# The experts' second products from rounded high and low parts, their weights split once and kept in DRAM

## The reference, cut to what matters

```python
logits = jnp.einsum('bnd,esd->bnes', x, phi)            # 4 experts, 256 slots each
dispatch = softmax(logits, axis=1)
combine = softmax(logits.reshape(B, N, E * S), axis=-1).reshape(B, N, E, S)
slots = jnp.einsum('bnd,bnes->besd', x, dispatch)
h = gelu(jnp.einsum('besd,edh->besh', slots, w1) + b1)   # tanh form, hidden width 768
y = jnp.einsum('besh,ehd->besd', h, w2) + b2             # the experts' second product
out = jnp.einsum('besd,bnes->bnd', y, combine)
```

## Time and profile before

| | |
|---|---|
| median of 3 runs | 876.32 us (874.78 to 877.62) |
| the profiled execution | 876.62 us, span 874.5 us |
| TensorE busy | 812.7 us (93%) |
| its weight loads | 661.5 us (76%) |
| VectorE busy | 458.6 us (52%) |
| ScalarE busy | 469.9 us (54%) |
| GpSimd busy | 185.9 us (21%) |
| moved by DMA | 15.58 MB |

### The profile page before, as it was taken

The page is one execution under the profiler, slowest core; times in us unless marked ns, Lnnn a source line. Parts: engine busy times, 40 slices in busy tenths (PEclk is TensorE's granted clock), DMA queues, the critical chain, the costliest instruction groups (busy, mean ns, idle before and its releaser), DMA issues.

```text
span 874.5 us, 14608 instructions
## 1 busy us (share of the span) xinstructions
PE 812.7 (93%) x5240; PEld 661.5 (76%) x5240; DVE 458.6 (52%) x1009; ACT 469.9 (54%) x961; POOL 185.9 (21%) x257
## 2 busy tenths in 40 slices
PE   1989989979998989989998999999999999999998
PEld 0866766666685669878887589976989589986988
DVE  4878697687877854566663730156102730155001
ACT  4968568568767733345654643455233633455132
POOL 3150022014000022235500530035000540035000
PEclk9989999999999979999999999999999999999999
DMA  7010000001000010001101100000000000000000
GB/s 211 1 30 14 1 16 24 0 0 36 0 1 1 1 45 12 12 13 49 38 1 64 64 1 1 1 18 0 0 0 18 0 0 0 0 18 1 1 1 19
DMA packets 12854, 15.58 MB, mean 18 GB/s; under 512 B 5328, under 2 KB 10704, under 8 KB 12688
## 3 DMA queue, kind: packets, MB, share of 16 engines
q1 hardware_dynamic: 10800, 9.56, 3.5%
q0 software_dynamic: 2016, 5.51, 2.2%
HBM read 13.49 MB, written 1.57 MB: 17 GB/s over the span
## 4 chain that ended last, share of the span: by engine, by line
PE 77%; DVE 9%; ACT 7%; issue 4%; DMA 1%; SPq 1%; POOL 0%; DVEq 0%; ACTq 0%; POOLq 0%
PE ps L221 19%; PE ps L1602 14%; PE ps L1517 6%; PE ps L1246 6%; PE ps L1617 5%; PE ps L1164 4%; PE ps L1336 4%; PE ps L1144 3%; DVE area L283 2%; ACT area L1066 2%; PE ps L1152 2%; ACT area L951 2%; PE ps L1124 1%; PE ps L1542 1%; PE ps L1204 1%
## 5 line engine op out<-in xcount | busy, mean ns | idle before, releaser
L1602 PE MATMUL ps<-area 128*128 128x192 f32 x768 | 127.4, 326 | 0.0
L1602 PEld LDWEIGHTS ps<-area 128*128 128x128 f32 x768 | 124.8, 190 | 2.0 <-issue 0.5
L221 PE MATMUL ps<-xs,ws 128*128 128x512 f32 x460 | 120.7, 412 | 5.4 <-DVE xs L511 3.7
L221 PE MATMUL ps<-ws,wx 128*128 128x512 f32 x480 | 116.1, 397 | 1.3 <-DVE ws L832 1.3
L1092 ACT ACTIVATE area<-ps,bcol 128x512 f32<-128x512 f32 x96 | 65.7, 689 | 86.6 <-PE ps L221 86.6
L843 DVE TENSOR_TENSOR area<-ps,area 128x384 f32<-128x384 f32 x32 | 17.9, 558 | 177.8 <-PE ps L1602 177.8
L221 PEld LDWEIGHTS ps<-ws,wx 128*128 128x128 f32 x480 | 89.2, 188 | 22.8 <-DVE ws L832 3.0
L221 PEld LDWEIGHTS ps<-xs,ws 128*128 128x128 f32 x460 | 87.0, 195 | 25.4 <-issue 6.6
L951 ACT ACTIVATE area<-ps,nm 112x196 f32<-112x196 f32 (+1 forms) x240 | 85.8, 442 | 19.5 <-DVE nm L646 19.5
L423 POOL TENSOR_TENSOR area<-area,dstat 128x512 f32<-128x512 f32 x32 | 38.0, 1198 | 250.7 <-DVE dstat L786 250.7
L646 DVE TENSOR_REDUCE nm<-ps 112x4 f32<-112x784 f32 (+1 forms) x72 | 62.7, 874 | 28.7 <-PE ps L1144 23.7
(11 more groups left out here) (176 smaller groups left out, 1339.7 us busy)
## 6 DMA issues: line engine op xcount, KB each, us to landing
stage<-in_wall POOLq DMA_DIRECT2D x42, 128.0 KB, 2.4
area<-in_w2e SPq DMA_DIRECT2D x1, 2304.0 KB, 8.4
out<-xres SPq DMA_DIRECT2D x4, 384.0 KB, 2.6
xres<-in_x SPq DMA_DIRECT2D x1, 1152.0 KB, 6.8
area<-in_wall SPq DMA_DIRECT2D x2, 512.0 KB, 6.2
area<-in_w2a SPq DMA_DIRECT2D x1, 576.0 KB, 3.8
room<-in_rel SPq DMA_DIRECT2D x4, 128.0 KB, 5.0
xres<-in_x SPq DMA_DIRECT2D x1, 384.0 KB, 3.2
```

The source lines that it names most:

```text
L221: last = mm(out_, l, r, start=n == 0, stop=n == len(pairs) - 1)
L1602: last = mm(ps[:, 4 + b, s * D:s * D + D], hTd[:, m, b * T + s * P:b * T + s * P + P], w2x[:, e * MC + m, :], start=m == 0, stop=m == MC - 1)
```

## The change

The gelu's result and the second weights are split in a rounded high part and the rounded rest. A second product of a tile becomes, for each of six blocks, one matmul of the high part with both parts of the weights side by side (384 columns) and one of the low part with the high weights (192 columns), all in float32r. The products with the high weights land in columns 0 to 191 of a PSUM bank, the product with the low weights in 192 to 383, and VectorE adds both to the bias in two additions (`add_up`). The product of the two low parts isn't computed.

ScalarE computes the gelu twice: once rounded to SBUF (`high`), once in full into the PSUM bank that held the hidden block, from which VectorE subtracts the high part to get `low`. The bank is free for the next hidden block only then. TensorE puts the first two hidden blocks of the next expert ahead of an expert's outputs. The parts have no room in SBUF for all experts: GpSimd loads the raw weights of an expert during each of the four rounds of the causal attention, splits them and writes both parts to DRAM (`keep_parts`), and SP fetches them for each expert of each pair into one of two buffers (`fetch_w2`). The scaling of the next images is put between the experts 0 and 1, the transposes for them behind the outputs of experts 2 and 3, and ScalarE's copies into expert 3 and behind it, ahead of the exponentials. The buffers `stage` and `area` get a second name in the rounded format at the same place. The diff, cut:

```diff
+        (dd, dt_, _, ct, bc, _, b2row) = views([
             (2, 2, NE * NS), (4, 2, T), (ST * 2,), (ST, N), (N,), (NE * MC, D), (NE, D)])
         yy = area[:, 0:2 * ST * (D + 1)].rearrange("p (b s d) -> p b s d", b=2, d=D + 1)
-        hTd = area[:, 2 * ST * (D + 1):2 * ST * (D + 1) + MC * N].rearrange("p (a b) -> p a b", b=N)
+        HAT = 2 * ST * (D + 1)
+        W2AT = 4 * NE * NS + 8 * T + 2 * ST + ST * N + N
+        w2s = rounded[:, W2AT:W2AT + NE * MC * D].rearrange("p (e c) -> p e c", e=2)
+        W2C = MC * 2 * D
+        raw = area[:, 0:MC * D].rearrange("p (m d) -> p m d", d=D)
+        parts = rounded[:, MC * D:MC * D + W2C]
+        w2_kept = nc.dram_tensor("w2_kept", [P, NE, W2C], F32, kind="Internal").ap()
+
+        def high(e, m):
+
+            v_ = xs[:, m, N:2 * N] if m < 2 and e % 2 else rounded[:, HAT + m * N:HAT + m * N + N]
+            return v_.rearrange("p (b t) -> p b t", b=2)
+
+        def low(e, m):
+
+            if m < 2 and e % 2:
+                return stage_r[:] if m else xs[:, 2, N:2 * N].rearrange("p (b t) -> p b t", b=2)
+            if m < 4:
+                return ws[:, 3, m * N:m * N + N].rearrange("p (b t) -> p b t", b=2)
+            return ws[:, 2 * m - 8:2 * m - 6, NE * 2 * NS:NE * 2 * NS + T]
         slots = [ws[:, k, 0:NE * 2 * NS] for k in range(3)]
...
             sp.wait_ge(o_res, 1 + 4 * PAIRS)
-            sp.dma_start(w2x, w2e).then_inc(ld_w2, 16)
-            sp.dma_start(b2row, b2r).then_inc(ld_w2, 16)
+            sp.dma_start(b2row, b2r).then_inc(ld_b2, 16)
+
+            def fetch_w2(k):
+
+                if k >= 2:
+                    sp.wait_ge(d_y, 1 + 4 * k)
+                sp.dma_start(w2s[:, k % 2].bitcast(F32), w2_kept[:, k % NE]).then_inc((ld_w2_even, ld_w2_odd)[k % 2], 16)
+
+            sp.wait_ge(w2_out, 16 * NE)
+            for k in range(2):
+                fetch_w2(k)
             for it in range(PAIRS):
+                for k in range(NE * it + 2, min(NE * it + 6, NE * PAIRS)):
+                    fetch_w2(k)
                 sp.wait_ge(d_res, 1 + NT * (it + 1))
...
+            def fetch_raw(e):
+
+                pool.dma_start(raw, w2e[:, e * MC:e * MC + MC, :]).then_inc(ld_raw, 16)
+
+            def keep_parts(e):
+
+                pool.wait_ge(ld_raw, 16 * (e + 1))
+                if e:
+
+                    pool.wait_ge(w2_out, 16 * e)
+                hi, lo = (parts.rearrange("p (m h d) -> p m h d", m=MC, h=2)[:, :, h, :] for h in range(2))
+                nc.gpsimd.tensor_copy(hi, raw).then_inc(w2_hi, 1)
+                pool.wait_ge(w2_hi, e + 1)
+                nc.gpsimd.tensor_tensor(lo, raw, hi.bitcast(F32), ALU.subtract).then_inc(w2_lo, 1)
+                pool.wait_ge(w2_lo, e + 1)
+                pool.dma_start(w2_kept[:, e], parts.bitcast(F32)).then_inc(w2_out, 16)
+                if e + 1 < NE:
+                    fetch_raw(e + 1)
+
             for ph in range(1, 4):
                 for n in range(PAIRS):
...
+                    if ph == 2:
+                        if n == 0:
+
+                            pool.wait_ge(b_res, 1 + 2 * PAIRS)
+                            fetch_raw(0)
+                        keep_parts(n)
             dispatch_combine(PAIRS - 1)
...
+
+            def add_up(it, e, g):
+
+                n = it * 4 * NE + 4 * e + g
+                dve.wait_ge(d_y, 5 + n + 1)
+                y_ = yy[:, g // 2, 2 * e + g % 2, 0:D]
+                V.tensor_tensor(y_, ps[:, 4 + g % 2, 0:D], b2row[:, e, :], ALU.add).then_inc(d_yo, 1)
+                dve.wait_ge(d_yo, n + 1)
+                V.tensor_tensor(y_, ps[:, 4 + g % 2, D:2 * D], y_, ALU.add).then_inc(d_ye, 1)
+
...
+                front = it + (3 * PAIRS + 1), it + 1, NT
                 if nxt:
-                    front_norm(it + (3 * PAIRS + 1), it + 1, NT, [(d_st, 1 + 4 * it + 4)])
+                    front_stats(*front)
                 for e in range(NE):
-                    for b in range(2):
-
-                        dve.wait_ge(d_y, 1 + it * 2 * NE + 2 * e + b + 1)
-                        if e + b == 0:
-                            V.memset(yy[:, :, :, D:D + 1], 1.0)
-                        V.tensor_tensor(yy[:, b, 2 * e:2 * e + 2, 0:D],
-                                        ps[:, 4 + b, 0:2 * D].rearrange("p (s d) -> p s d", d=D),
-                                        b2row[:, e, :].unsqueeze(1).broadcast_to([P, 2, D]), ALU.add).then_inc(d_ye, 1)
+                    for m in range(MC):
+                        n = it * NE * MC + e * MC + m
+
+                        dve.wait_ge(d_gelu, 1 + n + 1)
+                        V.tensor_tensor(low(e, m), ps[:, (e * MC + m) % 4, :].rearrange("p (b t) -> p b t", b=2),
+                                        high(e, m).bitcast(F32), ALU.subtract).then_inc(d_hl, 1)
+                        if e and m < 4:
+                            add_up(it, e - 1, m)
+                    if e == 0:
+                        dve.wait_ge(ld_b2, 16)
+                        V.memset(yy[:, :, :, D:D + 1], 1.0)
+                    if nxt and e < 2:
+                        front_scale(*front, range(2 * e, 2 * e + 2), [(d_st, 1 + 4 * it + 4)])
+                    if e == 3:
+                        for g in range(4):
+                            add_up(it, e, g)
                     if nxt and e == 3:
                         front_split(it + (3 * PAIRS + 1), NT, (d_l, ST * it + ST))
                 for k in range(2):
...
-                    if nxt and e in (1, 2):
-                        front_turned_part(it + (3 * PAIRS + 1), 0, e - 1)
-
-                    act.wait_ge(d_y, 1 + it * 2 * NE + 2 * e)
                     for m in range(MC):
+                        if nxt and e == 3 and m == 2:
+                            front_turned_part(it + (3 * PAIRS + 1), 0, 0)
                         act.wait_ge(d_h, it * NE * MC + e * MC + m + 1)
-                        A.activation(hTd[:, m, :], ps[:, (e * MC + m) % 4, :], ACT.Gelu_apprx_tanh,
-                                     bias=bcol[:, E1B + e * MC + m:E1B + e * MC + m + 1]).then_inc(d_gelu, 1)
+
+                        if m in (0, 2):
+                            act.wait_ge(d_y, (1 if m == 0 else 5) + it * 4 * NE + 4 * e)
+                        hidden = ps[:, (e * MC + m) % 4, :].rearrange("p (b t) -> p b t", b=2)
+                        bias = bcol[:, E1B + e * MC + m:E1B + e * MC + m + 1]
+                        A.activation(high(e, m), hidden, ACT.Gelu_apprx_tanh, bias=bias).then_inc(d_hh, 1)
+                        A.activation(hidden, hidden, ACT.Gelu_apprx_tanh, bias=bias).then_inc(d_gelu, 1)
+                if nxt:
+                    front_turned_part(it + (3 * PAIRS + 1), 0, 1)
                 for s in range(ST):
...
-                pe.wait_ge(ld_w2, 32)
                 pe.wait_ge(w_split, NCHUNK - QKV_CHUNKS)
                 pe.wait_ge(d_ss, 1 + it * 4 + 2)
+
+                def hidden(e, m):
+
+                    if e == 0 and m == 2:
+
+                        pe.wait_ge(d_ss, 1 + it * 4 + 4)
+
+                    pe.wait_ge(d_hl, it * NE * MC + e * MC + m + 1)
+                    product(ps[:, (e * MC + m) % 4, :], (CW1 + (e * MC + m) * P, CW1 + (e * MC + m) * P + P),
+                            scols(512 * e, 512 * e + 512)).then_inc(d_h, 1)
+
+                def outputs(e, g):
+
+                    b, s = g // 2, g % 2
+                    if 4 * e + g >= 2:
+
+                        pe.wait_ge(d_ye, 1 + it * 4 * NE + 4 * e + g - 1)
+                    to = ps[:, 4 + s, 0:2 * D]
+                    for m, part in ((0, 0), (0, 1), (1, 0), (1, 1), (2, 0), (2, 1), (3, 0), (3, 1), (4, 0), (4, 1), (5, 1), (5, 0)):
+                        w_ = w2s[:, e % 2, m * 2 * D:(m + 1) * 2 * D]
+                        if part == 0:
+                            if g == 0:
+                                pe.wait_ge(d_hh, it * NE * MC + e * MC + m + 1)
+                                gated(pe, 0)
+                            last = mm(to, high(e, m)[:, b, s * P:s * P + P], w_, start=m == 0, stop=m == MC - 1)
+                        else:
+                            if g == 0:
+                                pe.wait_ge(d_hl, 4 + it * NE * MC + e * MC + m + 1)
+                                gated(pe, 0)
+                            mm(to[:, 0:D], low(e, m)[:, b, s * P:s * P + P], w_[:, 0:D], start=False, stop=False)
+                    last.then_inc(d_y, 1)
+
                 for e in range(NE):
-                    for m in range(MC):
-                        if e == 0 and m == 2:
-
-                            pe.wait_ge(d_ss, 1 + it * 4 + 4)
-
-                        pe.wait_ge(d_gelu, 1 + it * NE * MC + max(0, e * MC + m - 3))
-                        product(ps[:, (e * MC + m) % 4, :], (CW1 + (e * MC + m) * P, CW1 + (e * MC + m) * P + P),
-                                scols(512 * e, 512 * e + 512)).then_inc(d_h, 1)
-
-                    pe.wait_ge(d_gelu, 1 + it * NE * MC + e * MC + MC - 1)
```

(59 more changed lines are left out.)

## The result

The changed kernel takes 892.5 us (median of 4 runs, 889.74 to 895.83); the kernel before, on the same chip, 876.97 (4 runs, 874.78 to 877.88). The ratio is 1.0189 [1.0165, 1.0213], which makes +16.6 us; the medians differ by 15.5. The forecast was 897. The profiled execution, the fastest of the four, took 889.74 us, with a span of 887.6 and a mean granted clock of 0.983.

The account below looks back on a forecast made before the run. TensorE, 77% of the chain that ended last, was taken to bound the kernel. Terms -15 + 2 + 5.6 + 3 + 12.3 + 10.8 + 2 = +20.7 on 876.6 us gave 897 us, range 882 to 908.

Parts of the forecast that it names:

- products, 16 experts: Experts' second products on TensorE: high plus low 286 ns against 325, an output block 6.86 us against 7.80; -15 us.
- waits in the first tile: First tile of an expert: waits ahead of every matmul may delay the next weight load; +2 us (0 to 19).
- expert 0, addition: Expert 0 of pairs with a successor: third tile's PSUM bank waits for VectorE's late first addition; +3 us.
- expert 3, last low part: Expert 3, without next hidden blocks before its outputs: TensorE waits 1.4 us for the last low part, four pairs; +5.6 us.
- end of a pair: Three pairs with a successor: ScalarE's copy delays the exponentials, so the combine waits; +4.1 us each, +12.3 us.
- splitting: Image attention: GpSimd's splitting delays rstd and VectorE's scaling by up to 12.3 us, less 1.3 lead; +10.8 us.
- clock: Six new TensorE waits, three in the attention and three at the combine, lower the granted clock; +2 us (0 to 8).
- rival 2: Second products: the weight load hides behind the neighbour's stream, 256 ns a pair, another -11.5 us, 886 us; chance 0.06.
- Rival 4: Image attention: DRAM copies collide with chunk loads and the clock falls for longer; 909 us; chance 0.06.
- Rival 3: Whole kernel: TensorE runs ahead of its helpers, so only its own work counts; 861.6 us, faster; chance 0.08.
- The signs named beforehand: Outputs near 6.9 us, exponentials 2.5 after them, TensorE idle 2.6 before combine, third rstd about 442, stage near 104 not 92.
- The sign against it: Expert stage: TensorE idle under 10 us would show the forecast wrong.

Follow-up runs that it names:

- run 3: Changed kernel with both transposes for the next images one expert earlier, behind the outputs of experts 1 and 2: 878.93 us, ratio 1.0029.
- runs 1 and 2: First: kernel before plus only GpSimd's splitting, parts unused, 889.27 us. Second: changed kernel, splitting one round later, chunks two a round from the MLP, 879.98 us.
- experiment 6: experiment 4 without the matmuls on the low part of the second products, waits kept: 833.25 us, ratio 0.9528 to the kernel before.
- experiment 5: Changed kernel with each part's splitting one round later in GpSimd's queue, chunks left as they are: 886.69 us, ratio 1.0142.
- experiment 4: Changed kernel with transposes one expert earlier, splitting one round later and chunks two a round from the MLP: 864.94 us, ratio 0.9875.

## Why the prediction was right

Step by step, in us, forecast against what traces and runs show:

| step | forecast | measured | from |
|---|---|---|---|
| products, 16 experts | -15 | -14.4 | 6.90 against 7.80 a block |
| waits in the first tile | +2 | 0 | same spacing of starts as elsewhere |
| expert 0, addition | +3 | 0 | additions of the first tile end at 525.20, the third tile starts at 525.81 |
| expert 3, last low part | +5.6 | +4.4 | 8.0 against 6.9, four times |
| end of a pair | +12.3 | +14.1 | 15.67, 16.08 and 15.17 against 10.95; run 3: 13.6 |
| splitting | +10.8 | +12.75 | stage; runs 1 and 2: 13.4 and 12.5 |
| clock | +2 | some 1.4, inside the end of a pair | two of the three combines at 0.50 |
| sum | +20.7 | +16.9 | medians +15.5, ratio +16.6 |

The direction and both large waits were right in place and cause. The forecast lay 4.5 us above the measured time, mainly because of two waits in the experts that didn't come.

**Products.** High plus low took 0.286 to 0.29 us as forecast, and by experiment 6 the split was right too: 173 to 175 and 113 to 115 ns against 171 and 115. In the mixed stream the time shows at the other product: from its start to the next one it is 200 ns for a high product behind a low one (176 behind a high one), and 88 ns for a low one ahead of a high one (medians over the changed kernel's mixture). The Trainium skill's rule on fast weight loads ("TensorE: Matmul & The Clock Gate", "Weight-path perf modes — Fast Weight Load (FWL) and DoubleRow"), read as rival 2 read it, asked for 256 ns a pair. The pair measured 286 to 290, and rival 2 is false.

**Waits inside an expert.** Two of the three were too dear, +5 us forecast and nothing found. The waits of the first tile had long been met when TensorE came to them, and even the weight loads lost nothing. For a block's two gelus the forecast took the 1.27 us of the earlier trace rows, which counts the whole of the second record: of the 1.27, 0.69 is one gelu, so the second started 0.58 us behind the first, and two take 1.16. ScalarE measured 1.15. In expert 0 its eight blocks so end at 524.49, 2.0 us behind TensorE's (522.52) and not 3.0, and VectorE's scaling took 1.1 us, not 1.35: the addition is ready 0.6 us early. Expert 3 was right in place and cost 1.1 instead of 1.4 us a pair.

**The end of a pair.** The exponentials began 2.55 us after the outputs' end (2.5 forecast), TensorE idled 2.7 (2.6), and the eight matmuls a tile then followed the exponentials, as worked out. Experiment 3 takes away only this and gains 13.6, so the mechanism is shown. The third pair, at full clock, cost 4.2 us, as forecast (4.1); the first two cost 4.7 and 5.1, and in their combines the granted clock was 0.50 from 573.5 to 576.9 and from 675.9 to 679.3, behind TensorE's idle 2.7 us. The difference most likely lies there; the forecast had let the exponentials cover it.

**The splitting.** Copy 1.15 and subtraction 2.61 us (1.2 and 2.7 forecast). With the hand-over and two issues a part takes 5.3 us (384.91 to 390.23), not 5.8. The first load was issued at 380.69 and used at 384.91, 4.2 us later (3.8 taken from the earlier trace rows), and the first scaling came 3.3 us late (3.2). The second and third were 11.0 and 13.3 late (9.8 and 12.3), counted from the start of the stage. So GpSimd set the pace, and the fourth round gave little back: its scaling, without a wait, was still 12.9 late. The forecast took 1.3 us of lead off the 12.3 (which makes 11.0, not 10.8); of the measured 13.3 only 0.5 was made up, so the lead was hardly there. In the third round VectorE waited only 0.82 us, because TensorE's chain ran slow too. Around the idle 3.63 us ahead of 394.79 and the 4.9 us ahead of 417.65, the granted clock was 0.68 and 0.77, between its levels of 1.2 and 2.4 GHz (stretch, us, busy us and records of TensorE, weight loads, VectorE, ScalarE, GpSimd; then clock, DMA share, GB/s):

```profile
384.00:400.00 16.00, 10.27 (x64) 8.01 (x62) 7.84 (x24) 7.30 (x16) 10.43 (x15) 0.68 0.40 132
415.00:430.00 15.00, 11.50 (x68) 9.65 (x69) 10.45 (x37) 5.78 (x14) 9.24 (x17) 0.77 0.40 125
```

It was at 0.50 from 389.2 to 399.4 and from 416.5 to 423.3; before the change, in this part of the stage, only from 394.2 to 397.6. Yet this adds nothing up to the third scaling: each of the three had an rstd as the last thing it waited for, so the clock's loss lies under GpSimd's. Where that cover is gone, as in experiment 5, it shows. Rival 4 is false: GpSimd waited 1.9 to 2.2 us for its chunk loads behind the stores, about as before, and 3.4 once; and the longer time at the lower clock was covered. The 16 fetches of an expert's parts cost nothing, as forecast; the page's part 6 gives 5.2 us each, with no wait for them (the 6.4 us of the raw loads is a median, and three of the four stand behind a store):

```profile
rounded<-w_kept SPq DMA_DIRECT2D x16, 1152.0 KB, 5.2
w_kept<-rounded POOLq DMA_DIRECT2D x4, 1152.0 KB, 5.5
area<-in_w2e POOLq DMA_DIRECT2D x4, 576.0 KB, 6.4
```

**Rival 3** (TensorE ahead of its helpers) is false for the change, and nearly true once two orders are put right: experiment 4 stands at 864.9, against its 861.6. The 3 us left are about expert 3's wait. So the arithmetic was worth what it promised, some 14 us; two steps that stood behind other work in an engine's queue took 26 to 28.

**The signs named beforehand.** The outputs (6.9 us), the exponentials' start (2.55), TensorE's idle time ahead of the combine (2.7), the third rstd (done at 438.25 in a trace that reaches the stage 4.5 us earlier, so 442.8 against 442) and the stage's lengthening (12.75 against 12) came as said. The sign against it, less than 10 us of TensorE idle in the expert stage, stayed away only just: the two new waits there are 8.2 + 2.5 = 10.7 us.

## What to carry to other kernels

When work is added to an engine that is nearly idle, ask first which small step of that engine others go straight on from, put the new work behind it, and see that a round still fits into the others' round: here 5.3 us of copies, four times ahead of a 1 us step, cost 12.5 us. The same copies behind it, with four chunks moved to an earlier stage, cost nothing that could be seen; behind it alone they still cost some 7 to 9. The same holds for a step that is moved: the copy of 0.6 us moved to the end of a pair held up 4.3 us of exponentials that had been hidden, and cost 4.2 to 5.1 each time. A second computation on a helper engine (96 gelus) cost only what lay at the one place without further TensorE work, 2 to 3 us of 67.

## What the runs showed of the hardware that was not expected

**The same idle time, and the lower clock for two different durations.** Ahead of the change's first instruction the profiled executions already differ by 4.5 us. Some 1.9 of them arise in the first 100 us: the kernel before ran at a granted clock of 0.50 from 49.5 to 56.3, the changed one at 1.00 there. The other 2.6 arise at the end of the windowed attention, where in both TensorE idles 2.22 us for VectorE. Stretches of the kernel before:

```profile
310.00:318.00 8.00, 5.23 (x16) 4.72 (x16) 3.15 (x10) 0.00 (x0) 0.00 (x0) 0.64 0.00 0
318.00:323.00 5.00, 4.72 (x12) 3.77 (x13) 3.22 (x13) 2.13 (x3) 3.21 (x6) 0.54 0.45 138
```

and of the changed kernel:

```profile
310.00:318.00 8.00, 6.82 (x26) 6.14 (x27) 2.61 (x11) 1.97 (x2) 0.88 (x2) 0.79 0.19 56
318.00:323.00 5.00, 5.00 (x25) 4.04 (x24) 3.99 (x9) 2.79 (x5) 3.81 (x7) 1.00 0.21 66
```

The first stays at 0.50 from 312.3 to 322.5 and needs 9.15 us for its next thirty products, from 318.28; the second is at 0.50 only from 310.7 to 314.1 and needs 7.20, from 315.73. The code is the same there. Over the 23 runs of the kernel before, the time goes with the mean granted clock: 872.2 to 873.7 us at 0.990 to 0.992, 875.8 to 878.3 at 0.981 and 0.982. So such stretches go along with much of the 3 to 6 us between runs of one kernel; what sets their length wasn't tried. It is the reason why a sum of terms is to be held against the medians, and against stages, rather than against two profiled spans.

**Which product of a pair the time shows at.** In a run of their kind, products of 192 columns start every 118 ns and those of 384 every 173 to 175. In turns, a pair takes 288: 200 from the long one's start to the short one's, and 88 from there to the next long one's. The short product is what costs 113 to 115 of them, though it takes up only 88 itself. Whether the weight loads are behind this isn't shown.
